# A graph attention layer with two paths: one block of five programs in place of two

## The reference

```python
Wh = X @ W.T                       # 8192 x 256
s_i = Wh @ r_src                   # r_src, r_dst: halves of r
s_j = Wh @ r_dst
e = s_i[:, None] + s_j[None, :]    # 8192 x 8192
e = jnp.where(e >= 0, e, 0.2 * e)
e = jnp.where(A == 0, -jnp.inf, e)
output = jax.nn.softmax(e, axis=1) @ Wh
x = layernorm(x + gelu(output), axis=-1)   # no scale or shift, eps 1e-5
```

## Time and profile before

| | |
|---|---|
| median of 3 runs | 1568.44 us (1567.83 to 1569.69) |
| the profiled execution, its own time | 1567.79 us |
| its span, first to last instruction | 1566.0 us |
| busy share of the span | PE 99%, DVE 95%, ACT 75%, POOL 29% |
| mean granted TensorE clock | 0.995 |

### The profile page before, as it was taken

How to read it: one execution, slowest core, us unless ns; L and a number is a source line. 1 busy time by engine, 2 the same in 40 slices (tenths; PEclk the granted TensorE clock), 3 DMA queues, 4 the chain that set the end, 5 groups by cost and what they waited for, 6 DMA issues and landing times.

```text
span 1566.0 us, 37044 instructions
## 1 busy us (share of the span) xinstructions
PE 1547.4 (99%) x12711; PEld 1535.3 (98%) x12711; DVE 1483.5 (95%) x1851; ACT 1178.5 (75%) x1528; POOL 460.7 (29%) x671
## 2 busy tenths in 40 slices
PE   9999999999999999999999999999999999999995
PEld 8899999999999999999999999999999999999995
DVE  5799999999999999999999999999999999999995
ACT  6767777777777777787777777778777777877773
POOL 1121233333323333322333332233333223333320
PEclk9999999999999999999999999999999999999998
DMA  9636687868588687858877785887777688777760
GB/s 209 121 56 87 92 117 101 113 88 126 73 126 118 101 109 93 121 75 126 115 106 104 97 117 78 128 111 108 102 102 115 80 127 106 105 106 104 108 94 28
DMA packets 295124, 164.16 MB, mean 105 GB/s; under 512 B 12320, under 2 KB 291104, under 8 KB 295072
## 3 DMA queue, kind: packets, MB, share of 16 engines
q0 software_dynamic: 278976, 142.12, 69.5%
q1 hardware_dynamic: 16096, 21.54, 5.0%
HBM read 289.41 MB, written 8.42 MB: 190 GB/s over the span
## 4 chain that ended last, share of the span: by engine, by line
PE 96%; issue 3%; POOL 0%; ACT 0%; DVE 0%; ACTq 0%; POOLq 0%
PE acc L760 31%; PE acc L750 30%; PE acc L753 30%; PE acc L698 3%; PE acc L686 1%; PE acc L720 0%; PE acc L664 0%; ACT P_hi L460 0%; POOL adj_in L257 0%; POOL rstd L310 0%; PE acc L728 0%; ACT Pw L349 0%; POOL rstd L334 0%; ACT gates L367 0%; ACTq L58 0%
## 5 line engine op out<-in xcount | busy, mean ns | idle before, releaser
L750 PE MATMUL acc<-WV_hi,P_hi 128*128 (+1 forms) x4096 | 997.4, 282 | 0.5 <-ACT P_hi L460 0.4
L753 PE MATMUL acc<-WV_lo,P_hi 128*128 (+1 forms) x4096 | 996.7, 281 | 0.0
L750 PEld LDWEIGHTS acc<-WV_hi,P_hi 128*128 128x128 f32 x4096 | 773.7, 189 | 1.1 <-ACT P_hi L460 0.8
L460 ACT CAST P_hi<-Pw 128x1024 fp32r<-128x1024 f32 x512 | 536.3, 1048 | 314.6 <-DVE Pw L576 157.5
L753 PEld LDWEIGHTS acc<-WV_lo,P_hi 128*128 128x128 f32 x4096 | 771.7, 188 | 0.0
L576 DVE SCALAR_TENSOR_TENSOR Pw<-R_row,X,gatesT 128x512 f32<-128x512 f32 x1024 | 709.9, 745 | 0.5 <-issue 0.5
L586 DVE TENSOR_TENSOR P_lo<-Pw,P_hi 128x1024 fp32r<-128x1024 f32 x512 | 624.3, 1219 | 37.8 <-ACT P_hi L460 35.1
L257 POOL DMA_DIRECT2D adj_in<-in_adj x512 | 330.2, 654 | 878.8 <-ACT gates L367 851.4
L760 PE MATMUL acc<-WV_hi,P_lo 128*128 (+1 forms) x4096 | 575.5, 283 | 0.0
L367 ACT ACTIVATE gates<-adj_in 128x1024 uint8<-128x1024 bf16 x512 | 536.8, 1048 | 31.1 <-DMA adj_in<-in_adj 24.6
L760 PEld LDWEIGHTS acc<-WV_hi,P_lo 128*128 128x128 f32 x4096 | 526.7, 189 | 0.0
(11 more groups left out here) (83 smaller groups left out, 221.1 us busy)
## 6 DMA issues: line engine op xcount, KB each, us to landing
adj_in<-in_adj POOLq DMA_DIRECT2D x512, 256.0 KB, 5.3
out<-y SPq DMA_DIRECT2D x64, 128.0 KB, 6.1
y<-in_x POOLq DMA_DIRECT2D x60, 128.0 KB, 6.0
Pw<-in_x SPq DMA_DIRECT2D x48, 128.0 KB, 3.9
R_row<-w_rows SPq DMA_DIRECT2D x15, 256.0 KB, 6.7
x_res<-in_x SPq DMA_DIRECT2D x20, 128.0 KB, 2.8
w_in<-in_L_gnn_W SPq DMA_DIRECT2D x1, 256.0 KB, 2.8
w_rows<-w_in SPq DMA_DIRECT2D x1, 32.0 KB, 2.1
```

Of the source, the lines that this page charges most:

```text
L460: nc.scalar.copy(P_hi[:, u % 2], Pw[u][:]).then_inc(s_hi, 1)
L750: nc.tensor.matmul(acc[r_][:, v, 0:HC], P_hi[:, u % 2, par, bass.ts(v, P)], WV_hi[:, k, :], start=(first and u == 0 and par == 0), stop=False)
L753: nc.tensor.matmul(acc[r_][:, v, 0:FOUT], P_hi[:, u % 2, par, bass.ts(v, P)], WV_lo[:, k, :], start=False, stop=False)
```

## The change

The two paths share one block. Each function now returns its five programs, and `layer` makes one block in which each engine runs its narrow program and then its general one. The block end between the paths is gone. In its place each engine drains at the end of its narrow part and adds 1 to a new semaphore, `s_done`. It then loads the verdict and takes the `If` at once, without waiting for another engine's end. What used to be ensured by the block end, that nobody begins the general path while another still works on the narrow one, is now a wait for `s_done` to reach 5, and it stands inside the `If`, so it is run only where the verdict is 0. The semaphores of both paths now live side by side; the tiles of the two paths use the same memory as before.

```diff
-def narrow_path(nc, x, adj, W, r, out, w_rows, taken):
+def narrow_path(nc, sems, x, adj, W, r, out, w_rows, taken, s_done):
...
         def sem(name):
-            return ctx.enter_context(nc.semaphore(name))
+            return sems.enter_context(nc.semaphore(name))
...
-        block = ctx.enter_context(nc.Block())
...
-        @block.sync
-        def _(sp):
+        def on_sync(sp):
...
             applies(sp, main)
+            sp.drain().then_inc(s_done, 1)
...
             applies(pool, main)
+            pool.drain().then_inc(s_done, 1)
...
             applies(act, main)
+            act.drain().then_inc(s_done, 1)
...
             applies(dve, main)
+            dve.drain().then_inc(s_done, 1)
...
             applies(pe, main)
-def general_path(nc, x, adj, W, r, out, taken=None):
+            pe.drain().then_inc(s_done, 1)
+        return on_sync, on_gpsimd, on_scalar, on_vector, on_tensor
+def general_path(nc, sems, x, adj, W, r, out, taken, s_done):
...
-        block = ctx.enter_context(nc.Block())
         def branch(eng, body):
-            if taken is None:
+            flag = eng.value_load(taken[0:1, 0:1], min_val=0, max_val=1)
+            with eng.If(flag == 0):
+                eng.wait_ge(s_done, 5)
                 body()
-            else:
-                flag = eng.value_load(taken[0:1, 0:1], min_val=0, max_val=1)
-                with eng.If(flag == 0):
-                    body()
...
-    with nc.sbuf_tensor("taken", [1, 1], I32) as taken:
-        narrow_path(nc, x, adj, W, r, out, w_rows, taken)
-        general_path(nc, x, adj, W, r, out, taken)
+    with ExitStack() as sems, nc.sbuf_tensor("taken", [1, 1], I32) as taken:
+        s_done = sems.enter_context(nc.semaphore("narrow_part_over"))
+        narrow = narrow_path(nc, sems, x, adj, W, r, out, w_rows, taken, s_done)
+        general = general_path(nc, sems, x, adj, W, r, out, taken, s_done)
+        block = sems.enter_context(nc.Block())
+        @block.sync
+        def _(sp):
+            narrow[0](sp)
+            general[0](sp)
...
+        @block.tensor
+        def _(pe):
+            narrow[4](pe)
+            general[4](pe)
```

More of the change, by code:

```diff
@@ L249, in _, with on_gpsimd @@
             applies(sp, main)
+            sp.drain().then_inc(s_done, 1)
         NP = NC // 2
-        @block.gpsimd
-        def _(pool):
+        def on_gpsimd(pool):
             def load(ah, r_, cp, i):
@@ L335, in _, with on_scalar @@
             applies(pool, main)
-        @block.scalar
-        def _(act):
+            pool.drain().then_inc(s_done, 1)
+        def on_scalar(act):
             act.sem_inc(s_g, 2 * RT)
@@ L480, in _, with on_vector @@
             applies(act, main)
-        @block.vector
-        def _(dve):
+            act.drain().then_inc(s_done, 1)
+        def on_vector(dve):
             nc.vector.memset(zeros, 0.0).then_inc(s_warm, 1)
@@ L657, in _, with on_tensor @@
             applies(dve, main)
-        @block.tensor
-        def _(pe):
+            dve.drain().then_inc(s_done, 1)
+        def on_tensor(pe):
             pe.sem_inc(s_free, 2)
@@ L798, in sem @@
         def sem(name):
-            return ctx.enter_context(nc.semaphore("g_" + name))
+            return sems.enter_context(nc.semaphore("g_" + name))
         ident = sb("ident", [P, P])
@@ L1071, in _ @@
             branch(pe, body)
+        return on_sync, on_gpsimd, on_scalar, on_vector, on_tensor
 def layer(nc, x, adj, W, r, out):
     w_rows = nc.dram_tensor("w_rows", (x.shape[0] // BANK, BANK), F32).ap()
-    with nc.sbuf_tensor("taken", [1, 1], I32) as taken:
-        narrow_path(nc, x, adj, W, r, out, w_rows, taken)
-        general_path(nc, x, adj, W, r, out, taken)
+    with ExitStack() as sems, nc.sbuf_tensor("taken", [1, 1], I32) as taken:
[7 more added lines that the diff above has]
+            general[0](sp)
+        @block.gpsimd
+        def _(pool):
+            narrow[1](pool)
+            general[1](pool)
+        @block.scalar
+        def _(act):
+            narrow[2](act)
+            general[2](act)
+        @block.vector
+        def _(dve):
+            narrow[3](dve)
+            general[3](dve)
+        @block.tensor
+        def _(pe):
+            narrow[4](pe)
+            general[4](pe)
 def kernel(**inputs):
```

## The result

The changed kernel takes 1565.32 us in the median of 20 runs (1563.19 to 1571.00), the kernel before 1569.58 in the median of 20 (1567.83 to 1575.53). The ratio is 0.9978, 95% interval 0.9971 to 0.9984: 0.22% faster, 3.5 us (2.5 to 4.6). The two medians lie 4.3 us apart and the two means 3.6; the ratio goes with the means. Forecast were 4.1 us or 0.26%.

What follows compares the result with a forecast made beforehand. TensorE bounds the main part; TensorE's late jump sets the end. SyncE's 1560.6 + 0.1 + 1.0 + 0.2 = 1561.9 against 1566.0 saves 4.1 us: 1568.44 - 4.1 = 1564.3 us, own range 1563.2 to 1565.2, whole 1562.6 to 1567.2.

Steps and rivals of the forecast that it cites:

- One late branch sets the end: After the last store lands: TensorE's 3,682 ns jump, held back by the first block end, sets the end of the span.
- TensorE's jump is hidden: End of span: TensorE, jumping early, is done at about 1554.7 us, hidden by the last block's finishing and the stores.
- The other engines are in time: End of span: ScalarE, VectorE and GpSimd stand at the end by about 1559.2 us; GpSimd's second drain takes 58 ns.
- SyncE's sum of 0.1 + 1.0 + 0.2: After the stores land at 1560.6: drain 0.1, load, arithmetic and jump 1.0, block end 0.2 us, ending at 1561.9.
- rival A: SyncE's jump after the stores: it takes the 3.7 us stall, uncovered; 0.4 us less than before, 1568.0 us; chance 0.09.
- No transfer is moved or added: Narrow path's end: the change moves or adds no transfer, and the stores still land at 1560.6 us.
- Both distances to the median unchanged: Execution 1.8 us above its span and median 0.65 above the execution both stay, so 1568.44 - 4.1 = 1564.3 us.
- rival B: Behind the span: code must be fetched in after the end, adding up to 1.8 us; 1566.1 us; chance 0.08.
- Rival C: TensorE's inner loop: new code layout exposes 132 ns at each of 96 branches, adding 12.7 us; 1577.0 us; chance 0.05.
- Rival D: End of span: an early jump gains nothing or engines still meet; only 0.4 us go, 1568.0 us; chance 0.06.

Runs made afterwards that it cites:

- e2: The changed kernel, but TensorE waits for all five narrow parts to be over before it loads the verdict; ratio to the kernel before 1.0003.
- e3: The kernel before with its two blocks, TensorE's program of the general path cut to one wait; ratio to the kernel before 0.9979.
- e8: The changed kernel with 600 more drains, never run, in SyncE's program inside the If; ratio to the kernel before 0.9994.
- e9: The changed kernel with VectorE's program of the general path cut to one wait; one run, 4.7 us from first of the last stores to end.
- e10: The changed kernel, but VectorE waits for all five narrow parts to be over before it loads the verdict; ratio to the kernel before 0.9979.
- e11: The changed kernel with SyncE's jump ahead of its store wait and VectorE's ahead of the last block's finishing; ratio to the kernel before 0.9972.
- e1: The changed kernel once more, unedited; ratio to the kernel before 0.9977.

## Why the prediction was right, and where it was off

- *One late branch sets the end*: right. Delaying it alone gives all back (e2), shortening it alone, without joining the blocks, saves 3.2 us (e3).
- *TensorE's jump is hidden*: right. It was over by 1556.4, 4.4 us behind TensorE's drain (4.6 forecast).
- *The other engines are in time*: right. GpSimd's second drain took 53 ns of the 58 allowed (and not 2.6 us), and it stood at the end at 1561.3, 3.2 us before SyncE.
- *SyncE's sum of 0.1 + 1.0 + 0.2*: right, 1.3 us behind the release. SyncE's own jump stayed at 50 ns, so rival A did not come about; where it was made to jump over a long body (e8) it cost 2.5 us and not 3.7.
- *"No transfer is moved or added"*: this step failed. I had read two packets of instruction fetch in the kernel before and given both to TensorE's stall. The one on q14 is VectorE's: it comes 1.2 us after VectorE's jump, vanishes with a short jump (e9) and moves with a late or early one (e10, e11). That jump now comes while the last stores are being issued, and its fetch holds the last pieces of the stores on one DMA engine for 0.9 us. The saving at the end is 8.8 - 5.5 = 3.3 us and not 4.1; the measured 3.5 us (2.5 to 4.6) fits either, so it is the traces of e9 and e10 that show it. That the two medians lie 4.3 us apart, close to the 4.1 of the forecast, is luck.
- *Both distances to the median unchanged*: the time outside the span stayed (1566.38 - 1564.7 = 1.7 us against 1.8), so rival B is out. The guess behind B had something to it: in the kernel before, TensorE's second fetch of 16 KB lies behind the span, from 1566.4 to 1567.7, and in the changed kernel it is over at 1558.5. The time outside the span is the same all the same, so that fetch isn't what fills it. But the median of 20 runs of the kernel before is 1569.58, not the 1568.44 of three. The forecast of 1564.3 would have been 1565.5 from there. The measured 1565.32 lies 0.1 us above the forecast's own range (1563.2 to 1565.2), inside the whole one. The luck of the front, 1.9 us between two profiles, is more than half of what the change is worth.
- *Rival C, the loops*: out. The stretch from the first to the last product of the main part is as long as before, 1467.1 us from the first product's start to the last one's end in both: the last products start 1.9 us later and so did the first.
- *Rival D*: out. The long wait for TensorE is gone in the changed kernel (0.2 us in place of 4.0) and in its repeat e1, and it is back when TensorE jumps late (e2).

What stays open: why the full clock is on record from 5 to 6.4 us on in some executions and from 10.7 to 13.8 in others, and where the 3.4 or 6.8 us at the lower level fall that some executions have later on and others don't. It happens to kernels with one block and with two, and no run was made on it.

## What to carry to other kernels

When the end of a span shows no busy engine, list the sequencers' instructions there one by one: a branch over code that is not run can cost microseconds (3.7 us here), and it should be taken by each engine as soon as that engine is idle, not behind a common barrier. Then ask what the earlier jump fetches and which transfer it will meet: here it delayed the last pieces of the stores by 0.9 us, and a last store has nothing behind it to hide a delay. For differences of a few tenths of a per cent, measure from a late event to the end in the trace; the run's whole time also holds what the clock did ahead of the main part, which here started anywhere from 82.9 to 85.4 us.

## What the runs showed of the hardware

- TensorE's jump over its long body took 3,323 to 3,758 ns in all joined kernels, wherever it was placed, and 226 ns over one wait (e3). The Trainium skill, page "Runtime: NRT & Kernel Launch", section "Instruction fetch mechanics", says that a taken branch whose target is not among the pages held waits for a fetch. The traces agree on TensorE: a fetch of 16 KB begins 1.0 to 1.1 us after each of the long jumps, and e3 has none.
- A halt may be booked behind a branch: 2.5 us on SyncE after a branch recorded with 50 ns (e8), 0.5 us on VectorE after one of 69 (e3).
- One fetch of 8 KB among 576 packets of stores delayed the last of them by 0.9 us (changed kernel against e9 and e10): nine packets came only after it was over. The fetch itself took 0.3 us alone (kernel before) and 0.8 among the stores.
